# Reordering one of four attention stages and the routed gathers in a fused attention and mixture-of-experts kernel

## The chip, the cores and the metric

The kernel runs on one core of one Trainium2 chip. The metric is the device time of the whole kernel in microseconds (us), lower is better. The engines are TensorE (PE in the profile), VectorE (DVE), ScalarE (ACT), GpSimd (POOL) and SyncE (SP), which here issues nearly all DMAs. TensorE's granted clock has two levels, 1.2 and 2.4 GHz; the profile's PEclk column gives it as a share of 2.4 GHz.

## The reference

One transformer block over 2048 tokens of width 512, in float32:

```python
h = _layernorm(x) * (1 + ca) + sa
x = x + ga * attention(h)          # 16 heads of 128, causal softmax
h = _layernorm(x) * (1 + cb) + sb
# router: softmax over 64 experts, the best 4 per token, at most 128 tokens per expert
yb = silu(xb @ Wg) * (xb @ Wu) @ Wd          # per expert
x = x + gb * (sum of a token's 4 weighted expert rows + shared experts(h))
```

`sa, ca, ga, sb, cb, gb` come from a small matrix product of a conditioning vector. Two shared experts with 512 hidden columns each run over all tokens beside the routed ones.

## The kernel before, in words

**Precision.** A float32 product is made of three matmuls on a high and a low part of each operand (`matmul3`, lines 1559 to 1561). Whatever leaves PSUM therefore leaves it twice: ACT writes the high part, then DVE writes what is missing to the full value as the low part.

**Attention.** Heads run one after the other. A head has four blocks of 512 queries (j = 0 to 3), and causality gives block j the keys of blocks 0 to j. The unit of work is a stage (h, j); every engine has its own `stage` function with its orders written out by hand, and engines meet through semaphores. PE's stage (line 1649) does three things: `score(h, j)`, the logits of block j in strips of up to 512 columns (4 rows of j+1 strips, in four PSUM banks `strip`); `sum_values` of the stage before, the product of its probabilities and the values, in j+1 groups of 512 keys into the bank `pv`; and `project` for the next stage: queries, keys and values (q, k, v) into the three banks `gen`. After block 3 comes block 0 of the next head, whose stage is (h+1, 0): it holds the scores of block 0, the four-group sum of block 3 of the head before, and the projections of block 1. "The fourth block's sum" is that sum. A loop of 15 turns holds the stages (h,1), (h,2), (h,3), (h+1,0); stage (0,0) stands in front of it.

DVE's `score_row` (line 1141) takes a row of strips out of PSUM with its maximum, and ACT's `exp_row` (line 852) exponentiates it. `row_inverse` (DVE, line 1160) inverts the sum, `probs_hi` (ACT, line 858) and `probs_lo` (DVE, line 1168) make the two float16 halves of the probabilities. `gen_hi_of` (ACT, line 836) and `gen_out_of` (DVE, line 1112) take the projections out. The probabilities and the values have to be transposed for `sum_values`; that is done by DMA transposes, issued one after the other by SP (`turn_pair`, line 469, and `turn_values`, line 495).

Four orders matter around the change. (a) A pair of transposed groups goes into one of four slots of `pT`. Block 0 of a head uses slot 0, which group 2 of the fourth block's sum has to leave first: `turn_first_rows` (line 475) waits for `pv_group`, `slot_free`. (b) In SP's stage for j = 0 come the four transposes of block 0's probabilities, then `turn_values(h, 0)`, the transpose of block 0's values. (c) There is one buffer `vT16` for values before their transpose. ACT may write the values of block 1 into it only once the values of block 0 have been transposed out of it, which `gen_hi_of` says for v:

```python
act.wait_ge(v_turned, h * (16 * QB) + 16 * j)
```

(d) ACT does `gen_hi_of("v")` at the end of stage (h, 0), ahead of the exponentials of stage (h, 1), and DVE's `gen_out_of("v")` waits for it.

**After attention.** The output projection; a second layer norm; then shared-expert chunks 0 to 2 (12 steps of `shared_units`) with the router's steps beside them, given by the table `ROUTING` (line 421). Its last entry, `("table", 1)`, writes the table of routed tokens. On it wait SP's first expert weights, POOL's first gather of token rows (lines 796 to 798) and PE's first expert. 64 experts follow, with chunks 3 and 4 between them. Then come chunks 5 to 7, 12 more steps of `shared_units` (PE: gate, half of the down product of the step before, up, the other half), and beside them the combine: POOL gathers each token's four expert rows (line 811, four indirect DMAs per tile of 128 tokens, four buffers `gath`), and DVE's `combine_beside` (line 1526) adds them with their weights to the output (line 1541), two tiles in a step, in the steps that the table `COMBINE` names (line 410). PE's down product of a step waits for DVE's `shared_lo` (`hs_lo`, line 1360), which stands behind the combine of the step before on DVE.

Of the kernel before, what the change touches and what calls it, by code (L numbers as in the profile page):

```python
# [21 lines left out]
U32 = mybir.dt.uint32  # L22
ALU = mybir.AluOpType
ACT = mybir.ActivationFunctionType
AX_X = mybir.AxisListType.X
P = 128
# [15 lines left out]
def adaln_block(nc, x, Q_w, Q_b, K_w, K_b, V_w, V_b, O_w, O_b, Wr, router_bias, Wg, Wu, Wd, Sg, Su, Sd,  # L42
# [22 lines left out]
    with ExitStack() as ctx:  # L65
        def sem(name):
            return ctx.enter_context(nc.semaphore(name))
# [160 lines left out]
        slot_now = f.place("slot_now", [P, GATHS, TOPK], U32)  # L228
# [93 lines left out]
        slot_ready = sem("slot_ready")  # L322
# [83 lines left out]
        def raw_of(c):  # L406
# [3 lines left out]
        COMBINE = {step: pair for pair, step in enumerate((2, 3, 4, 6, 7, 8, 9, 10))}  # L410
# [13 lines left out]
                   11: [("table", 1)]}  # L424
# [245 lines left out]
        def _(pool):  # L670
# [133 lines left out]
            with pool.Fori(0, NT // GATHS) as g:  # L804
                for i in range(GATHS):
                    wait_alone(gath_free, g * GATHS + (i + 1))
                    nc.gpsimd.tensor_copy(slot_now[:, i, :], slot_u[:, bass.ds(g * GATHS + i, 1), :]
                                          .rearrange("p o k -> p (o k)")).then_inc(slot_ready, 1)
                    wait_alone(slot_ready, g * GATHS + (i + 1))
                    for k in range(TOPK):  # L810
                        nc.gpsimd.indirect_dma_start(
                            out=gath[i][:, k, :], out_offset=None, in_=yb_dram,
                            in_offset=bass.IndirectOffsetOnAxis(ap=slot_now[:, i, k:k + 1], axis=0)
                        ).then_inc(g_landed[i], 16)
# [3 lines left out]
        def _(act):  # L818
# [61 lines left out]
            def stage(h, j, prev, nxt):  # L880
                if nxt is not None and nxt[1] == 0:

                    act.wait_ge(gen_out, nth("v", QB - 1, h) + GENS)
                    for n in range(3):
                        act.wait_ge(raw_landed[n], h * 16 + 32)
                        if n == 2:
                            act.wait_ge(abs_ready, h + 1)
                        split_hi(n)
                exp_row(h, j, 0)
                exp_row(h, j, 1)  # L890
                probs_hi(h, j, prev, 0)
                probs_hi(h, j, prev, 1)
                exp_row(h, j, 2)
                exp_row(h, j, 3)
                probs_hi(h, j, prev, 2)
                probs_hi(h, j, prev, 3)
                if prev is not None:
                    attended(*prev)
                if j == 0:
                    take_at_scale(h)  # L900
                if nxt is not None:
                    for kind in "qkv":
                        gen_hi_of(kind, nxt[1], nxt[0])
# [156 lines left out]
        def _(dve):  # L1060
# [80 lines left out]
            def score_row(h, j, t):  # L1141
                for ch in range(j + 1):
# [31 lines left out]
            def stage(h, j, nxt):  # L1174
                score_row(h, j, 0)
                score_row(h, j, 1)
                row_inverse(h, j, 0)
                score_row(h, j, 2)
                row_inverse(h, j, 1)
                score_row(h, j, 3)  # L1180
                probs_lo(h, j, 0)
                row_inverse(h, j, 2)
                probs_lo(h, j, 1)
                row_inverse(h, j, 3)
                probs_lo(h, j, 2)
                probs_lo(h, j, 3)
                if nxt is not None:
                    hn, jn = nxt
                    gen_out_of("q", jn, hn)
                    gen_out_of("k", jn, hn)  # L1190
                    if jn == 0:
                        value_scale(hn, pv[:, 0:1])
                    gen_out_of("v", jn, hn)
# [335 lines left out]
            def combine_beside(step):  # L1529

                if step not in COMBINE:
                    return
                pair = (2 * COMBINE[step], 2 * COMBINE[step] + 1)
                dve.wait_ge(down_out, OUT_AFTER + step // (SC - AFTER0) * TB)
                for k in range(TOPK):
                    for t in pair:
                        if k == 0:
                            dve.wait_ge(g_landed[t % GATHS], (t // GATHS + 1) * 16 * TOPK)
                        else:
                            dve.wait_ge(dve_step, steps[0] - 1)  # L1540
                        ins = nc.vector.scalar_tensor_tensor(acc[:, t, :], gath[t % GATHS][:, k, :],  # L1541
                                                             w_top[:, t, k:k + 1], acc[:, t, :], ALU.mult, ALU.add)
                        steps[0] += 1
                        ins.then_inc(dve_step, 1)
                dve.wait_ge(dve_step, steps[0])
                dve.sem_inc(combined, 2)
                dve.sem_inc(gath_free, 2)
# [8 lines left out]
        def _(pe):  # L1556
# [81 lines left out]
            def stage(h, j, prev, nxt):  # L1638
                score(h, j)
                if prev is not None:  # L1640
# [4 lines left out]
                if nxt is not None:  # L1645
                    hn, jn = nxt
                    project("q", jn, hn)
                    project("k", jn, hn)
# [263 lines left out]
```

## Time and profile before

| | us |
|---|---|
| median of 3 runs | 2115.48 (2110.93 to 2117.49) |
| profiled execution, own time | 2119.06 |
| its span | 2117.3 |
| PE busy | 2014.0 (95%) |
| DVE busy | 1381.3 (65%) |
| ACT busy | 1103.8 (52%) |
| POOL busy | 386.7 (18%) |

Attention takes the span from about 70 to 1375 us, the output projection goes on to 1590, chunks 0 to 2 with the router to 1700, the experts to 1988, chunks 5 to 7 with the combine to the end. In a timeline a row gives start, duration, engine, line and operation, output and inputs with their shapes, and in brackets how long the engine sat idle before it and what ended that. Matmuls are pipelined: one of 512 columns is shown with some 0.39 us but the next starts 0.23 us later, so start to start is the thing to read. In a table of stretches the number in brackets behind a busy time is the number of instructions.

### The profile page before, as it was taken

To read this page: it belongs to the slowest core of one execution; us is meant where nothing else is said; L and a number is where in the kernel's file an instruction comes from. 1 tells how busy PE (TensorE), PEld (TensorE's weight loads), DVE (VectorE), ACT (ScalarE), POOL (GpSimd) and SP (SyncE) were. 2 spreads that over 40 slices of the span, in tenths; PEclk is the share of its full clock that TensorE was granted. 3 is DMA by queue.
4 is the path that set the end of the run, shared out by engine and by line. 5 is a ranking of instruction groups with operands and counts; after the bars stand their busy time and mean duration, and the time that the engine had idled before them with its cause. 6 is when DMAs were issued, how large, how long until landed. Compare 5 with 4: busy or idle time off the path is not lost.

```text
span 2117.3 us, 33076 instructions
## 1 busy us (share of the span) xinstructions
PE 2014.0 (95%) x9863; PEld 1501.2 (71%) x9865; DVE 1381.3 (65%) x3219; ACT 1103.8 (52%) x1638; POOL 386.7 (18%) x409
## 2 busy tenths in 40 slices
PE   6899999999999999999999999999999989999997
PEld 4667667676676677676676776667877768777775
DVE  7677686686686686776866866846545833333375
ACT  3566575676575575665766755623333134444310
POOL 5211010010110110110100101633000132222364
PEclk8999999999999999999999999999999999999998
DMA  6488888888888878878888888994431098989664
GB/s 214 95 162 161 162 162 162 162 162 161 159 165 162 173 151 171 166 156 165 162 162 161 162 161 164 214 212 151 129 106 30 1 299 286 312 279 324 187 191 152
DMA packets 932173, 366.06 MB, mean 173 GB/s; under 512 B 754800, under 2 KB 885920, under 8 KB 932128
## 3 DMA queue, kind: packets, MB, share of 16 engines
q1 hardware_dynamic: 921888, 331.93, 69.5%
q0 software_dynamic: 10240, 33.56, 5.2%
q8 instruction: 25, 0.41, 0.1%
q14 instruction: 20, 0.16, 0.0%
HBM read 138.86 MB, written 41.94 MB: 85 GB/s over the span
## 4 chain that ended last, share of the span: by engine, by line
PE 65%; SPq 15%; DMA 8%; DVE 4%; issue 4%; POOL 3%; ACT 1%; DVEq 0%; POOLq 0%; ACTq 0%
SPq L473 14%; PE gen L1559 9%; PE gen L1561 9%; PE gen L1560 9%; PE strip L1559 7%; PE strip L1560 6%; PE strip L1561 6%; PE strip L1851 4%; PE pv L1559 4%; PE pv L1561 3%; PE pv L1560 3%; DMA wd_sb<-in_L_ffn_Wd 3%; DMA pT<-p_lo 2%; PE strip L1858 2%; DVE acc L1541 1%
## 5 line engine op out<-in xcount | busy, mean ns | idle before, releaser
L1171 DVE SCALAR_TENSOR_TENSOR p_lo<-exps,rinv,p_hi 128x512 f16<-128x512 f32 (+3 forms) x256 | 395.4, 1560 | 27.9 <-ACT p_hi L864 24.3
L855 ACT ACTIVATE exps<-exps,nbias 128x128 f32<-128x128 f32 (+15 forms) x256 | 306.3, 1197 | 136.7 <-DVE nbias L1157 136.7
L864 ACT ACTIVATE p_hi<-exps,rinv 128x512 f16<-128x512 f32 (+3 forms) x256 | 338.1, 1351 | 15.1 <-DVE rinv L1166 6.7
L1559 PE MATMUL strip<-kT_hi,qT_hi 128*128 128x512 f32 (+3 forms) x640 | 238.3, 372 | 14.4 <-DVEq L1248 6.3
L1147 DVE TENSOR_SCALAR_CACHE_REDUCE exps<-strip 128x512 f32<-128x512 f32 x384 | 249.1, 685 | 1.8 <-PE strip L1561 1.8
L1559 PE MATMUL pv<-pT,v 128*128 128x512 f16 (+3 forms) x640 | 223.3, 349 | 21.0 <-DMA pT<-p_lo 19.7
L1560 PE MATMUL strip<-kT_lo,qT_hi 128*128 128x512 f32 (+3 forms) x640 | 234.4, 366 | 0.0
L1561 PE MATMUL strip<-kT_hi,qT_lo 128*128 128x512 f32 (+3 forms) x640 | 234.1, 366 | 0.0
L710 POOL TENSOR_TENSOR wq_lo<-wq_raw,wq_hi 128x512 fp32r<-128x512 f32 x16 | 20.8, 1300 | 1105.2 <-ACT wq_hi L834 1105.2
L1560 PE MATMUL pv<-pT,v 128*128 128x512 f16 (+3 forms) x640 | 222.1, 347 | 0.0
L1561 PE MATMUL pv<-pT,v 128*128 128x512 f16 (+3 forms) x640 | 218.8, 347 | 0.0
L1559 PEld LDWEIGHTS strip<-kT_hi,qT_hi 128*128 128x128 f32 x640 | 121.2, 189 | 47.0 <-DVE exps L1147 14.9
L1031 ACT ACTIVATE xbT<-gen,modT,scale_b 128x128 f32<-128x128 f32 x256 | 96.1, 456 | 92.0 <-PE gen L1843 92.0
L1559 PEld LDWEIGHTS pv<-pT,v 128*128 128x128 f16 x640 | 62.4, 97 | 114.8 <-DMA pT<-p_lo 49.2
L1561 PEld LDWEIGHTS strip<-kT_hi,qT_lo 128*128 128x128 f32 x640 | 121.3, 190 | 19.1
L1560 PEld LDWEIGHTS strip<-kT_lo,qT_hi 128*128 128x128 f32 x640 | 121.7, 190 | 15.4
L1117 DVE SCALAR_TENSOR_TENSOR qT_lo<-gen,bias_now,qT_hi 128x512 fp32r<-128x512 f32 x64 | 47.8, 746 | 126.8 <-ACT qT_hi L841 126.8
L1124 DVE SCALAR_TENSOR_TENSOR vT<-gen,v_scale,vT 128x512 f16<-128x512 f32 x64 | 48.0, 750 | 122.8 <-ACT vT L849 122.8
L1153 DVE CUSTOM_DVE_ANT_0 exps<-strip,causal 128x128 f32<-128x128 f32 (+3 forms) x256 | 124.5, 486 | 5.2 <-PE strip L1561 1.1
L1499 DVE TENSOR_TENSOR hE<-strip,sil_e 128x128 f32<-128x128 f32 x64 | 18.6, 291 | 157.2 <-ACT sil_e L1038 98.0
L849 ACT ACTIVATE vT<-gen,v_scale 128x512 f16<-128x512 f32 x64 | 44.0, 687 | 134.1 <-PE gen L1561 130.3
L1559 PE MATMUL gen<-hT_hi,a_hi 128*128 128x512 f32 x256 | 100.7, 394 | 9.1 <-DVE a_lo L1290 7.6
(237 smaller groups left out, 4433.5 us busy)
## 6 DMA issues: line engine op xcount, KB each, us to landing
at_dram<-at_f SPq DMA_DIRECT2D x64, 256.0 KB, 2.6
wg_sb<-in_L_ffn_Wg SPq DMA_DIRECT2D x64, 256.0 KB
wu_sb<-in_L_ffn_Wu SPq DMA_DIRECT2D x64, 256.0 KB
wd_sb<-in_L_ffn_Wd SPq DMA_DIRECT2D x64, 256.0 KB
yb_dram<-yb SPq DMA_DIRECT2D x64, 256.0 KB
a_f<-at_dram SPq DMA_DIRECT2D x58, 256.0 KB, 2.9
pT<-p_hi SPq DMA_TRANSPOSE x320, 3.3
pT<-p_lo SPq DMA_TRANSPOSE x320, 3.3
```

Of the source, the lines that this page charges most:

```text
L473: sp.dma_start_transpose(out, rows).then_inc(p_turned[slot_of(j, g)], 16)
L855: nc.scalar.activation(row, row, ACT.Exp, bias=nbias[:, t:t + 1], accum_out=rsum[:, t:t + 1]).then_inc(row_probs, 1)
L864: nc.scalar.activation(p_hi16[:, 0:j + 1, t, :], row, ACT.Copy, scale=rinv[:, t:t + 1]).then_inc(p_hi, 1)
L1031: ins = nc.scalar.activation(xbT[:, i % 2, P * ch:P * ch + P], e_turn[:, P * ch:P * ch + P], ACT.Identity, bias=modT[:, 3 * DC + ch:3 * DC ...
L1124: ins = nc.vector.scalar_tensor_tensor(vT16[:, 1, :], src[:], v_scale[:, 0:1], vT16[:, 0, :], ALU.mult, ALU.subtract)
L1147: nc.vector.tensor_scalar(exps[:, t, 512 * ch:512 * ch + w], strip[u % STRIPS][:, 0:w], SCALE, None, ALU.mult, ALU.max, accum_out=cmax[:, ...
L1153: nc.vector.tensor_tensor_reduce(exps[:, t, 512 * ch:512 * ch + w], strip[u % STRIPS][:, 0:w], causal[:, TB * P - w:TB * P], SCALE, -3e38, ...
L1171: nc.vector.scalar_tensor_tensor(p_lo16[:, 0:j + 1, t, :], row, rinv[:, t:t + 1], p_hi16[:, 0:j + 1, t, :], ALU.mult, ALU.subtract).then_i ...
L1559: nc.tensor.matmul(o, a_hi, b_hi, start=start, stop=False)
L1560: nc.tensor.matmul(o, a_hi, b_lo, start=False, stop=False)
L1561: return nc.tensor.matmul(o, a_lo, b_hi, start=False, stop=stop)
L1851: last = nc.tensor.matmul(e_gateup[i % 2][:, P * n:P * n + P], w[:, i % EX, c, :], xbT[:, i % 2, P * c:P * c + P], start=c == 0, stop=c == ...
```

## The change

It has four parts.

1. Stage (h, 0) on PE, ACT and DVE: q and k of block 1 are projected between the scores of block 0 and the fourth block's sum; v stays behind the sum. ACT takes q and k out ahead of its four `probs_hi`, and DVE ahead of its four `probs_lo`. SP's order is as before.
2. Stage (h, 1) on DVE: the first score row comes ahead of the low part of v of block 1 (`gen_out_of("v", 1, h)`), with a wait on `p_lo` in `score_row` for j = 1.
3. The table of routed tokens is read in step 10 instead of step 11.
4. The gathers at the end are written out tile by tile and take their indices from `slot_u` directly, without a copy to `slot_now` and a wait on it. The combine follows a new schedule from step 1 to step 10, tile by tile, each operation waiting for the one before, and frees a buffer after each tile.

```diff
-        COMBINE = {step: pair for pair, step in enumerate((2, 3, 4, 6, 7, 8, 9, 10))}
+        COMBINE = {1: (0, 1), 2: (2, 3), 3: (4,), 4: (5, 6), 5: (7, 8), 6: (9,), 7: (10, 11), 8: (12, 13), 9: (14,),
+                   10: (15,)}
...
-                   11: [("table", 1)]}
+                   10: [("table", 1)]}
...
-            with pool.Fori(0, NT // GATHS) as g:
-                for i in range(GATHS):
-                    wait_alone(gath_free, g * GATHS + (i + 1))
-                    nc.gpsimd.tensor_copy(slot_now[:, i, :], slot_u[:, bass.ds(g * GATHS + i, 1), :]
-                                          .rearrange("p o k -> p (o k)")).then_inc(slot_ready, 1)
-                    wait_alone(slot_ready, g * GATHS + (i + 1))
-                    for k in range(TOPK):
-                        nc.gpsimd.indirect_dma_start(
...
+            for t in range(NT):
+                pool.wait_ge(gath_free, t + 1)
+                for k in range(TOPK):
+                    nc.gpsimd.indirect_dma_start(
+                        out=gath[t % GATHS][:, k, :], out_offset=None, in_=yb_dram,
+                        in_offset=bass.IndirectOffsetOnAxis(ap=slot_u[:, t, k:k + 1], axis=0)
+                    ).then_inc(g_landed[t % GATHS], 16)
...
                 exp_row(h, j, 0)
                 exp_row(h, j, 1)
-                probs_hi(h, j, prev, 0)
-                probs_hi(h, j, prev, 1)
-                exp_row(h, j, 2)
-                exp_row(h, j, 3)
-                probs_hi(h, j, prev, 2)
-                probs_hi(h, j, prev, 3)
+                if j == 0:
+                    exp_row(h, j, 2)
+                    exp_row(h, j, 3)
+                    gen_hi_of("q", nxt[1], nxt[0])
+                    gen_hi_of("k", nxt[1], nxt[0])
+                    for t in range(TB):
+                        probs_hi(h, j, prev, t)
+                else:
...
                 if j == 0:
                     take_at_scale(h)
-                if nxt is not None:
+                    gen_hi_of("v", nxt[1], nxt[0])
+                elif nxt is not None:
...
             def score_row(h, j, t):
+                if j == 1:
+                    dve.wait_ge(p_lo, h * NT + (t + 1))
...
             def stage(h, j, nxt):
                 score_row(h, j, 0)
+                if j == 1:
+                    gen_out_of("v", 1, h)
                 score_row(h, j, 1)
                 row_inverse(h, j, 0)
                 score_row(h, j, 2)
                 row_inverse(h, j, 1)
                 score_row(h, j, 3)
...
+                if j == 0:
+                    row_inverse(h, j, 2)
+                    row_inverse(h, j, 3)
+                    gen_out_of("q", nxt[1], nxt[0])
+                    gen_out_of("k", nxt[1], nxt[0])
+                    probs_lo(h, j, 0)
+                    probs_lo(h, j, 1)
...
+                    if jn != 1:
+                        gen_out_of("v", jn, hn)
...
-                pair = (2 * COMBINE[step], 2 * COMBINE[step] + 1)
                 dve.wait_ge(down_out, OUT_AFTER + step // (SC - AFTER0) * TB)
-                for k in range(TOPK):
-                    for t in pair:
...
-                dve.wait_ge(dve_step, steps[0])
-                dve.sem_inc(combined, 2)
-                dve.sem_inc(gath_free, 2)
+                for t in COMBINE[step]:
+                    dve.wait_ge(g_landed[t % GATHS], (t // GATHS + 1) * 16 * TOPK)
+                    for k in range(TOPK):
+                        link(nc.vector.scalar_tensor_tensor(acc[:, t, :], gath[t % GATHS][:, k, :], w_top[:, t, k:k + 1],
+                                                            acc[:, t, :], ALU.mult, ALU.add))
+                    dve.sem_inc(combined, 1)
+                    dve.sem_inc(gath_free, 1)
...
             def stage(h, j, prev, nxt):
                 score(h, j)
+                if j == 0:
+                    project("q", *reversed(nxt))
+                    project("k", *reversed(nxt))
...
                     sum_values(hp, jp)
                 if nxt is not None:
                     hn, jn = nxt
-                    project("q", jn, hn)
-                    project("k", jn, hn)
+                    if j > 0:
+                        project("q", jn, hn)
+                        project("k", jn, hn)
```

## Rows read from the trace of the kernel before

**Rows 1.** Table of stretches, the 15 turns of the attention loop

```profile
core 0: us, PE busy (x) PEld busy (x) DVE busy (x) ACT busy (x) POOL busy (x), PEclk, DMA share, GB/s
120.00:1375.00 1255.00, 1227.60 (x5898) 883.96 (x5896) 929.11 (x2415) 804.92 (x1046) 138.00 (x116) 1.00 0.84 165
```

**Rows 2.** Timeline of PE, one stage (h, 0) and the scores behind it

```profile
639.24 0.40 PE L1561 MATMUL strip<-kT_hi,qT_lo 128*128 128x512 f32 x1
639.67 0.39 PE L1559 MATMUL pv<-pT,v 128*128 128x512 f16 x1
...
647.65 0.38 PE L1561 MATMUL pv<-pT,v 128*128 128x512 f16 x1
649.21 0.39 PE L1559 MATMUL pv<-pT,v 128*128 128x512 f16 x1 [1.18 <-DMA pT<-p_lo]
...
650.82 0.47 PE L1559 MATMUL gen<-hT_hi,wq_hi 128*128 128x512 f32 x1
...
659.09 0.39 PE L1559 MATMUL strip<-kT_hi,qT_hi 128*128 128x512 f32 x1
...
661.50 0.50 PE L1559 MATMUL strip<-kT_hi,qT_hi 128*128 128x512 f32 x1 [0.19 <-DVE exps L1147]
...
664.24 0.39 PE L1559 MATMUL pv<-pT,v 128*128 128x512 f16 x1
```

**Rows 3.** Timeline of SP's queue in the same stage, the transpose of block 0's values

```profile
654.08 1.23 SPq L499 DMA_TRANSPOSE v<-vT  x1
```

**Rows 4.** Timelines of SP, ACT and PE in stage (0, 0), by time

```profile
79.11 0.69 ACT L843 ACTIVATE kT_hi<-gen,bias_now 128x512 fp32r<-128x512 f32 x1 [1.20 <-PE gen L1561]
...
80.34 1.28 SPq L499 DMA_TRANSPOSE v<-vT  x1
...
83.50 0.69 ACT L849 ACTIVATE vT<-gen,v_scale 128x512 f16<-128x512 f32 x1 [3.71 <-DMA v<-vT]
...
85.64 0.50 PE L1559 MATMUL strip<-kT_hi,qT_hi 128*128 128x512 f32 x1 [1.79 <-DVE exps L1147]
```

**Rows 5.** DMA issues with their median us from issue to landing

```profile
at_dram<-at_f SPq DMA_DIRECT2D x64, 256.0 KB, 2.6
...
v<-vT SPq DMA_TRANSPOSE x64, 3.1
```

**Rows 6.** Timeline of PE, the first matmul behind three long waits

```profile
1426.70 0.50 PE L1559 MATMUL gen<-hT_hi,a_hi 128*128 128x512 f32 x1 [3.11 <-DVE a_lo L1290]
...
2043.77 0.79 PE L1559 MATMUL strip<-s_hi,hs_hi 128*128 128x512 f32 x1 [3.24 <-DVE hs_lo L1360]
...
2083.92 0.69 PE L1559 MATMUL strip<-s_hi,hs_hi 128*128 128x512 f32 x1 [4.06 <-DVE hs_lo L1360]
```

**Rows 7.** Table of stretches that begin at these matmuls (columns as in rows 1)

```profile
1426.70:1433.00 6.30, 4.72 (x19) 3.58 (x20) 6.23 (x7) 0.84 (x2) 6.30 (x5) 1.00 0.85 284
...
2043.80:2050.80 7.00, 7.00 (x18) 5.51 (x19) 1.38 (x2) 0.00 (x0) 4.95 (x7) 0.57 0.76 236
2083.90:2088.90 5.00, 4.98 (x15) 3.98 (x16) 0.54 (x1) 0.00 (x0) 3.58 (x5) 0.66 0.98 339
```

**Rows 8.** Timelines of DVE and PE where the table is read and the experts begin

```profile
1696.65 0.22 DVE L1479 CAST table<-strip 128x64 int32<-128x64 f32 x1
...
1704.78 0.83 PE L1843 MATMUL gen<-ident,xb 128*128 128x128 f32 x4 [4.94 <-DMA xb<-n_dram,tok_now]
```

**Rows 9.** POOL's timeline; the tile gath (ns min/median/max, first and last start us)

```profile
2088.79 0.95 POOL L811 DMA_INDIRECT gath<-yb_dram,slot_now  x1 [0.30 <-issue]
...
L811 POOL DMA_INDIRECT gath<-yb_dram,slot_now x64: 942/972/1505, 1993.9 to 2097.6; - x64
L1541 DVE SCALAR_TENSOR_TENSOR acc<-gath,w_top,acc x64: 742/744/792, 2013.6 to 2105.3; 128x512 f32<-128x512 f32 x64
```

**Rows 10.** Timeline of PE: gate of step 2, gate of step 6, last down product

```profile
2004.61 0.39 PE L1559 MATMUL strip<-h2T_hi,s_hi 128*128 128x512 f32 x1
...
2037.58 0.39 PE L1559 MATMUL strip<-h2T_hi,s_hi 128*128 128x512 f32 x1
...
2108.56 0.79 PE L1559 MATMUL strip<-s_hi,hs_hi 128*128 128x512 f32 x1 [4.79 <-DVE hs_lo L1360]
```

More of the change, by code:

```diff
@@ L227, in adaln_block @@
         ones_bf = f.place("ones_bf", [P, P], BF16)
-        slot_now = f.place("slot_now", [P, GATHS, TOPK], U32)
         tok_now = f.place("tok_now", [P, EX], I32)
@@ L321, in adaln_block @@
         yb_stored = [sem(f"yb_stored{i}") for i in range(EX)]
-        slot_ready = sem("slot_ready")
         g_landed = [sem(f"g_landed{i}") for i in range(GATHS)]
@@ L803, in _ @@
                 pool.wait_ge(yb_stored[i], 16 * (E // EX + 1))
-            with pool.Fori(0, NT // GATHS) as g:
-                for i in range(GATHS):
-                    wait_alone(gath_free, g * GATHS + (i + 1))
-                    nc.gpsimd.tensor_copy(slot_now[:, i, :], slot_u[:, bass.ds(g * GATHS + i, 1), :]
-                                          .rearrange("p o k -> p (o k)")).then_inc(slot_ready, 1)
-                    wait_alone(slot_ready, g * GATHS + (i + 1))
-                    for k in range(TOPK):
-                        nc.gpsimd.indirect_dma_start(
-                            out=gath[i][:, k, :], out_offset=None, in_=yb_dram,
-                            in_offset=bass.IndirectOffsetOnAxis(ap=slot_now[:, i, k:k + 1], axis=0)
-                        ).then_inc(g_landed[i], 16)
+            for t in range(NT):
[5 more added lines that the diff above has]
+                    ).then_inc(g_landed[t % GATHS], 16)
         @block.scalar
@@ L890, in stage @@
                 exp_row(h, j, 1)
-                probs_hi(h, j, prev, 0)
-                probs_hi(h, j, prev, 1)
-                exp_row(h, j, 2)
-                exp_row(h, j, 3)
-                probs_hi(h, j, prev, 2)
-                probs_hi(h, j, prev, 3)
+                if j == 0:
[6 more added lines that the diff above has]
+                else:
+                    probs_hi(h, j, prev, 0)
+                    probs_hi(h, j, prev, 1)
+                    exp_row(h, j, 2)
+                    exp_row(h, j, 3)
+                    probs_hi(h, j, prev, 2)
+                    probs_hi(h, j, prev, 3)
                 if prev is not None:
@@ L1180, in stage @@
                 score_row(h, j, 3)
[L1181 to L1184, printed above, removed]
+                if j == 0:
[5 more added lines that the diff above has]
+                    probs_lo(h, j, 1)
+                else:
+                    probs_lo(h, j, 0)
+                    row_inverse(h, j, 2)
+                    probs_lo(h, j, 1)
+                    row_inverse(h, j, 3)
                 probs_lo(h, j, 2)
@@ L1188, in stage @@
                     hn, jn = nxt
-                    gen_out_of("q", jn, hn)
-                    gen_out_of("k", jn, hn)
+                    if j > 0:
+                        gen_out_of("q", jn, hn)
+                        gen_out_of("k", jn, hn)
                     if jn == 0:
                         value_scale(hn, pv[:, 0:1])
-                    gen_out_of("v", jn, hn)
+                    if jn != 1:
+                        gen_out_of("v", jn, hn)
             def ln_stat_of(b):
@@ L1532, in combine_beside @@
                     return
-                pair = (2 * COMBINE[step], 2 * COMBINE[step] + 1)
                 dve.wait_ge(down_out, OUT_AFTER + step // (SC - AFTER0) * TB)
-                for k in range(TOPK):
-                    for t in pair:
[L1537 to L1544, printed above, removed]
-                dve.wait_ge(dve_step, steps[0])
-                dve.sem_inc(combined, 2)
-                dve.sem_inc(gath_free, 2)
+                for t in COMBINE[step]:
[5 more added lines that the diff above has]
+                    dve.sem_inc(gath_free, 1)
             for c in (6, 7):
@@ L1646, in stage @@
                     hn, jn = nxt
-                    project("q", jn, hn)
-                    project("k", jn, hn)
+                    if j > 0:
+                        project("q", jn, hn)
+                        project("k", jn, hn)
                     if jn == 0:
```

## The prediction

> **What bounds the kernel now.** I read the table of stretches first, then PE's timeline, then the queue that feeds it. In the attention loop PE is busy for 1227.60 of 1255 us at full clock [rows 1]: only PE's waits, some 2 us in a head, can be won there, and any new wait of PE costs in full. PE's timeline of a stage (h, 0) shows those waits. The sum of block 3 runs from 639.67 to 650.82, and in front of its last group PE waits for a transposed probability tile (1.18 us in the row; 1.34 beyond the pitch of 0.2155 us at which its matmuls follow each other); its other groups and its start wait 0.1 to 0.3 us each. The scores of block 1 then wait 0.36 us for a free strip at 661.50, because DVE had the values' low part to do first [rows 2]. At the end, chunks 5 to 7, PE waits again and again for DVE's `hs_lo`, up to 4.79 us [rows 6, 10], as DVE is in a combine that waits for gathers.
>
> **Part 1 and 2, attention.** The three waits go, about 2.1 us a head. But the projections of q and k are put ahead of the sum, so everything behind the sum is late by their time, and SP's chain is behind the sum: block 0's transposes need the slot that group 2 leaves, block 0's values come after them, and ACT may write block 1's values only when those have landed. Step by step, from the last score matmul at 639.24:
>
> - q, k and v are 36 matmuls, 650.82 to 659.09 [rows 2], 8.27 us; q and k are two thirds, 5.5, v is 2.75. Scores end at 639.47, q and k at 644.98.
> - Groups 0 to 2 of the sum: last matmul 647.65 - 639.67 = 7.98 after the first, less the small waits 0.4 [rows 2]: 7.6. So it starts at 652.58 instead of 647.65. The whole sum is 11.15 less 1.7 of waits = 9.4, and ends at 654.4. The last group's tiles, there by 649.2 [rows 2], are no longer late.
> - From that matmul to the issue of the value transpose: 654.08 - 647.65 = 6.43 [rows 2, 3], four transposes and the sequencer's steps. Nothing is taken out of it, so the issue is at 659.0. The probabilities are not what it waits for: ACT's high parts move behind k, which PE has done at 645.0, and 4 us are enough for them.
> - From issue to ACT writing block 1's values. Stage (0, 0) of this trace shows exactly this wait: 83.50 - 80.34 = 3.16, with "3.71 <-DMA v<-vT" [rows 4]. So ACT writes at 662.2; the projection of v was done at 657.2. DVE's low part stands behind it, and behind that score row 1, whose first strip is the one PE needs next.
> - From ACT's write to PE's next free strip: 85.64 - 83.50 = 2.14 [rows 4]: 664.3.
>
> PE meanwhile ran v (to 657.15) and scores: row 0 is now taken out early, so PE gets through six of eight strips, 2304 of 3328 columns of the 4.7 us that the scores take without their wait [rows 2], to 660.4, and then stands until 664.3, **3.9 us**. Two strips remain: 2.74 us from 661.50 to 664.24 for 1920 columns, so 1.46 for 1024 [rows 2]. The next sum begins at 665.8, against 664.24: **+1.5 us a head, where the waits removed are worth -2.4**. What runs behind it (ACT's and DVE's rows of block 1, about 1.7 late) keeps its distance to PE, so nothing is given back. 15 turns: **+23 us**. The bounds of this term: landing 3.0 to 3.5 instead of 3.16 and SP's reaction 0.1 shorter give +1.3 to +2.0 a head, 20 to 30 us.
>
> The Trainium skill (Advanced Engine Details and Errata, X-Bar Transpose (TRN2)) says that transposing DMAs are as fast as regular ones. Here a plain store of 256 KB lands after 2.6 us and the value transpose after 3.1 [rows 5], so the trace does not quite agree; by the page it would be 0.5 us less a head, +15 instead of +23.
>
> Stage (0, 0) has no sum in it. PE's order is the same, but ACT makes k's high part (79.11 + 0.69 [rows 4]) and only then the first two high halves, which SP's transposes follow. The value transpose, now at 80.34 [rows 4], comes about 6.4 later, at 86.7, and a PE strip follows 5.3 us behind it (85.64 - 80.34), at 92.0: 6.4 later than 85.64, of which about 1.2 come back, since two strips are left then instead of four. **+5 us**, once; bounds 3 and 8.
>
> **The clock.** A stand of 3.9 us costs more than itself. Of three waits of its size, two (3.24 and 4.06) were followed by a stretch at a granted clock of 0.57 and 0.66, that is partly at the 1.2 GHz level; the third (3.11) by 1.00 [rows 6, 7]. The time lost is 7.0 x 0.43 = 3.0 and 5.0 x 0.34 = 1.7 [rows 7]. Here the stretch behind the wait is all PE, so it is lost in full. The new wait is nearer to 4.06 than to 3.11. I take 1.8 us a head, near the row of 4.06; bounds 0 and 3.0. 15 heads and the first stage: **+29 us**, bounds 0 and 48.
>
> The wait on `p_lo` in DVE's row 0 costs nothing: the value waited for was written 8 us before by DVE itself. PSUM banks and q's registers are free in time, since scores precede the new projections on PE.
>
> **Part 3, the table.** It is read at 1696.65, after step 11's `hs_lo` [rows 8]. What it is made of is complete in step 10, and a step is 8.2 us (below): the read comes nearly 8 us earlier. PE's first expert at 1704.78 waited 4.94 us for the gathered rows [rows 8]; they come as much earlier, so the wait goes, but the sums of step 11 and ACT's split of chunk 4 are late next and keep about 1.5 us. Against it stands the half clock after that wait, about 1.7 as in the row of 2083.9 [rows 7]. **-5 us**, bounds -3 and -7; the experts behind it follow as a whole.
>
> **Part 4, gathers and combine.** Undisturbed, chunks 5 to 7 go at (2037.58 - 2004.61) / 4 = 8.24 us a step [rows 10]. Step 11 would begin at 2004.61 + 9 x 8.24 = 2078.8, its up product end 6.9 later and its low part 2.4 behind that: last down product at 2088.2 instead of 2108.56 [rows 10], and at full clock 2.8 long instead of 5.1. So at most -22.7 is to be had. A gather takes 0.95 + 0.30, at most 1.5 + 0.30 beside DVE's work, with a median near the short end [rows 9]: four to a tile are 5.0 to 5.5 without the copy and its waits, where all 64 now take 1993.9 to 2097.6, 6.5 a tile [rows 9]. The first goes some 2 us earlier without its copy; 16 tiles are issued by 2072 to 2079, and freed buffers come in time. DVE's chain costs 4 x 0.78 = 3.1 us a tile (0.744 [rows 9] and the wait for itself), two tiles 6.2 against 5.4 now. Going through the steps with 5.4 a tile, tile 8 (step 5) and tile 13 (step 8) land some 2 us after DVE wants them, and each makes PE wait about 1.8 us; the others are in time. That takes back 3.7, and 1 us more if the clock falls once: **-18 us**, bounds -22.7 and -10.
>
> **Sum.** +23 + 5 + 29 - 5 - 18 = +34 us against the profiled execution's 2119.06, which is 3.6 above the median of the runs shown. Against the median, 2115.5, the forecast is **2149 us** (+1.6%).
>
> **Rivals.** What a measurement of this kernel can tell from no change is about 0.3%, 6.3 us.
>
> (A) The forecast, chance 0.60: PE stands nearly 4 us in each stage (h, 1), with a clock drop behind most of them.
>
> (B) The same wait, but the clock holds, as it did after 3.11 us [rows 7]: +5 in all, 2120 us. Chance 0.14. For it: that one row, and that PE is dense on both sides of this wait. Against: the other two [rows 6, 7].
>
> (C) The value transpose is not late, the faster side. It decides at a landing of block 0's values by 660.4, when PE has run through its six strips, less the 2.14 of ACT and DVE: so at 658.3 instead of 662.2. If SP's transposes of block 0 did not follow group 2, they would go out from 648.3 on as now, and the waits of 2.1 + 0.3 us go: 15 x -2.4 = -36, -5, -18: 2056 us. Against it stand the wait on the slot in the code and the fact that SP starts these transposes only after group 2. Chance 0.09.
>
> (D) More of it, chance 0.17: two half-clock stretches behind each stand (the 3.0 of the 2043.8 row), or late gathers that hold PE as now, so that part 4 brings 8 instead of 18. +50 to +60, 2165 to 2175 us.
>
> **Range and chances.** From 2116, the lower edge of (B) where part 4 brings its full 22.7, to 2168, within (D); (C) and the upper part of (D) are left out. Slower by over 0.3%: (A), (D) and the half of (B) above 2122: 0.83. Within 0.3%: the rest of (B) and a little: 0.08. Faster: 0.09.
>
> **What would show it.** In the changed kernel: ACT's `vT` of block 1 ended by "DMA v<-vT" in all 16 heads, instead of once; the value transpose issued some 5 us later after the scores; a PE wait of 3.5 to 4 us in the scores of block 1, ended by DVE's `exps`, with PEclk below 1.00 in the loop's stretch; the waits for `pT` gone from the sum; a period of about 85.4 us a head instead of 82.1. The table read a step earlier, PE's first expert without its 5 us; the last down product some 20 us nearer to the first gate. I am wrong if the head's period is below 82 (then C), or if it is about 83.7 with a clock of 1.00 (then B).

## The result, and the profile after

The changed kernel takes **2163.53 us** (median of 4 runs, 2156.50 to 2167.07) where the kernel before took 2113.20 beside it: a ratio of 1.023, 95% interval 1.020 to 1.027. The forecast was 2149 (2116 to 2168), slower. Direction and range held; below it is seen that one term had the wrong sign, and another, too large, covered for it.

| profiled execution | before | after |
|---|---|---|
| time, span, us | 2119.06, 2117.3 | 2167.07, 2165.3 |
| mean granted clock | 0.989 | 0.976 |
| a head, us (ACT's `at_scale`, first to last, / 15) | 82.21 | 85.05 |
| read of the table, us | 1696.65 | 1736.68 |
| first expert's matmul, us | 1704.78 | 1748.26 |
| first gather's issue, us | 1993.9 | 2030.2 |
| last down product, us | 2108.56 | 2158.98 |

**The attention loop.** The same stretch as [rows 1], of the changed kernel (columns as there), and ACT's `at_scale`, which is written once a head (count, ns min/median/max, first to last start in us):

```profile
120.00:1375.00 1255.00, 1203.88 (x5733) 869.18 (x5732) 901.19 (x2329) 780.12 (x1022) 109.95 (x93) 0.98 0.81 158
```

```profile
L872 ACT ACTIVATE at_scale<-v_most x16: 191/203/203, 81.9 to 1357.6; 128x1 f32<-128x1 f32 x16
```

PE's busy share of the stretch falls by 24 us and the clock from 1.00 to 0.98. (1357.6 - 81.9) / 15 = 85.05 us a head. One stage (h, 0) and the scores behind it, by time: PE, then SP, then ACT and DVE of the changed kernel.

```profile
662.06 0.40 PE L1572 MATMUL strip<-kT_hi,qT_lo 128*128 128x512 f32 x1
...
683.10 0.34 PE L1572 MATMUL strip<-kT_hi,qT_lo 128*128 128x384 f32 x1
686.80 0.50 PE L1570 MATMUL strip<-kT_hi,qT_hi 128*128 128x512 f32 x1 [3.37 <-DVE exps L1153]
...
688.40 0.63 PE L1572 MATMUL strip<-kT_hi,qT_lo 128*128 128x512 f32 x1
```

```profile
675.80 1.24 SPq L472 DMA_TRANSPOSE pT<-p_hi  x1
...
679.96 1.27 SPq L472 DMA_TRANSPOSE pT<-p_lo  x1
681.56 1.23 SPq L498 DMA_TRANSPOSE v<-vT  x1
```

```profile
684.67 0.69 ACT L844 ACTIVATE vT<-gen,v_scale 128x512 f16<-128x512 f32 x1 [6.06 <-DMA v<-vT]
...
685.39 0.75 DVE L1128 SCALAR_TENSOR_TENSOR vT<-gen,v_scale,vT 128x512 f16<-128x512 f32 x1 [3.42 <-ACT vT L844]
686.06 0.68 DVE L1153 TENSOR_SCALAR_CACHE_REDUCE exps<-strip 128x512 f32<-128x512 f32 x1
```

The reader is to follow it backwards: PE's strip at 686.80 waited for DVE's `exps` of 686.06, that stood behind the values' low part, that waited for ACT's high part, and that for the transpose issued at 681.56, behind the four of the probabilities. The last of PE's rows shows the half clock: a matmul of 512 columns has a row of 0.63 us there, instead of 0.39. Two of the 15 stretches behind such a stand:

```profile
686.80:691.80 5.00, 5.00 (x19) 2.92 (x20) 4.74 (x18) 4.48 (x7) 0.00 (x0) 0.66 0.76 188
348.10:353.10 5.00, 4.99 (x26) 3.66 (x27) 4.74 (x18) 4.48 (x7) 0.00 (x0) 1.00 0.75 188
```

13 of the 15 heads look like the first (5.0 x 0.34 = 1.7 us lost), two like the second. What the waits of the whole program show of it:

```profile
DVE vT L1128 <- ACT vT L844: 150.5, 62, 6.5
DVE exps L1153 <- PE strip L1572: 132.5, 16, 8.9
ACT vT L844 <- DMA v<-vT: 99.0, 16, 7.6
PE strip L1570 <- DVE exps L1153: 57.9, 16, 6.8
PE strip L1570 <- DVE hs_lo L1378: 29.5, 5, 16.8
DVE sil_s L1374 <- remote: 26.1, 4, 11.3
ACT sil_s L990 <- remote: 14.6, 3, 7.2
```

ACT waits for the landing 16 times instead of once; PE's 57.9 us for `exps` were 4.7; PE's waits for `pT` in the sum, 19.7 us before, are gone. The last three rows belong to the end.

**The table and the end.** PE's timeline at the first expert, of the changed kernel; the 4.94 us of [rows 8] are gone:

```profile
1748.26 0.65 PE L1858 MATMUL gen<-ident,xb 128*128 128x128 f32 x4 [0.45 <-issue]
```

From the first gate's neighbourhood to the last down product the change was to save 18 us, and it lost some. Nothing of [rows 6, 10] is as long as what stands there now (timelines of PE, ACT, DVE and POOL, by time):

```profile
2049.45 0.39 PE L1572 MATMUL gen<-h2T_hi,s_lo 128*128 128x512 f32 x1
2051.86 0.69 DVE L1374 TENSOR_TENSOR sil_s<-gen,sil_s 128x512 f32<-128x512 f32 x1 [1.69 <-remote]
...
2053.62 0.39 PE L1572 MATMUL strip<-h2T_hi,s_lo 128*128 128x512 f32 x1
...
2058.06 0.39 PE L1572 MATMUL strip<-h2T_hi,s_lo 128*128 128x512 f32 x1
2059.01 0.60 ACT L990 ACTIVATE sil_s<-strip 128x512 f32<-128x512 f32 x1 [5.80 <-remote]
...
2073.27 0.95 POOL L806 DMA_INDIRECT gath<-yb_dram,slot_u  x1 [0.30 <-issue]
2074.57 0.69 DVE L1374 TENSOR_TENSOR sil_s<-strip,sil_s 128x512 f32<-128x512 f32 x1 [11.32 <-remote]
2079.43 0.77 PE L1570 MATMUL strip<-s_hi,hs_hi 128*128 128x512 f32 x1 [16.85 <-DVE hs_lo L1378]
...
2082.73 0.95 POOL L806 DMA_INDIRECT gath<-yb_dram,slot_u  x1 [8.51 <-DVEq L1558]
```

The up product's last matmul starts at 2058.06 and ACT's silu is done at 2059.6; DVE's product of the two needs nothing else and starts at 2074.57. "Remote" is the page's word for a wait whose end it can put down to nobody: the signal came, but whoever gives it had ended long before. In these 16 us POOL issues gathers 1.25 us apart (0.95 + 0.30) without a break, as it has done since 2030.2, up to 2074.2. The longer it does so, the later the signals are. PE's last matmuls in the rows end 0.39 us after their starts, at 2049.84, 2054.01 and 2058.45; the instructions that wait for them (DVE at 2051.86, ACT at 2059.01, DVE at 2074.57) start 2.0, 5.0 and 16.1 us after that. A second long wait of this kind (9.93 us) ends at 2131.65, 2.4 us after POOL's last gather. The gathers themselves are as fast as forecast.

### The profile page after: what moved, and what is told of

Read it like the earlier page. It is cut to its first block, busy times and chain, and to the rows that moved or that the text cites. A ratio compares the mean times of both kernels' runs of the same rounds, so it can differ in the third digit from the quotient of the medians.

```text
span 2165.3 us, 33071 instructions
## 1 busy us (share of the span) xinstructions
PE 2022.7 (93%) x9865; PEld 1507.4 (70%) x9865; DVE 1389.9 (64%) x3219; ACT 1103.4 (51%) x1638; POOL 381.8 (18%) x393
## 4 chain that ended last, share of the span: by engine, by line
PE 74%; SPq 7%; DMA 6%; DVE 6%; issue 2%; POOL 2%; another core or an unknown queue 1%; ACT 1%; DVEq 0%; ACTq 0%; POOLq 0%
PE gen L1570 10%; PE gen L1572 10%; PE gen L1571 10%; PE strip L1570 7%; PE strip L1572 6%; PE strip L1571 6%; SPq L472 5%; PE pv L1570 5%; PE pv L1571 5%; PE pv L1572 5%; PE strip L1866 4%; DMA v<-vT 2%; DMA wd_sb<-in_L_ffn_Wd 2%; PE strip L1873 2%; DVE acc L1555 2%
## 5 line engine op out<-in xcount | busy, mean ns | idle before, releaser
L1570 PE MATMUL strip<-kT_hi,qT_hi 128*128 128x512 f32 (+3 forms) x640 | 240.5, 376 | 67.6 <-DVE exps L1153 57.9
L1570 PE MATMUL pv<-pT,v 128*128 128x512 f16 (+3 forms) x640 | 229.9, 359 | 0.0
L1571 PE MATMUL pv<-pT,v 128*128 128x512 f16 (+3 forms) x640 | 228.6, 357 | 0.0
L1572 PE MATMUL pv<-pT,v 128*128 128x512 f16 (+3 forms) x640 | 224.4, 356 | 0.0
L1572 PEld LDWEIGHTS strip<-kT_hi,qT_lo 128*128 128x128 f32 x640 | 122.8, 192 | 19.6
L1571 PEld LDWEIGHTS strip<-kT_lo,qT_hi 128*128 128x128 f32 x640 | 122.8, 192 | 15.5
L1570 PEld LDWEIGHTS pv<-pT,v 128*128 128x128 f16 x640 | 64.6, 101 | 81.1 <-issue 22.2
L1572 PEld LDWEIGHTS pv<-pT,v 128*128 128x128 f16 x640 | 64.4, 101 | 61.3 <-issue 5.5
```

Of the source, the lines that this page charges most:

```text
L1570: nc.tensor.matmul(o, a_hi, b_hi, start=start, stop=False)
L1571: nc.tensor.matmul(o, a_hi, b_lo, start=False, stop=False)
L1572: return nc.tensor.matmul(o, a_lo, b_hi, start=False, stop=stop)
```

## The experiments

Three theories stood after the trace. **T1**: the landing of block 0's values is the new wait, SP's place behind the sum makes it late, and the half clock follows from PE's stand. **T2**: POOL's unbroken issue holds up PE's signals to DVE and ACT. **T3**, the rival to T2: the new combine, or chance. Ratios are to runs of the kernel before on the same chip, times are medians.

### Attention alone, the end alone

`attn_only` is the kernel before with the diff's attention part; `end_only` has the rest (table in step 10, COMBINE by tile, gathers written out).

> Edit: the kernel before with parts 1 and 2 (the attention's order) alone; table, gathers and combine as before. My reading of the changed kernel's trace: a head takes 85.0 us instead of 82.1, so 15 x 2.9 = 44, and the first stage some 5: 2160 to 2166 us, nothing like a 10 us stall behind 1990 us. Rival (parts 3 and 4 bring the 23 us of the forecast, and the attention costs 73): 2183 to 2190. Rival (the attention costs only what was forecast without the clock, 28): 2141.

> Edit: the kernel before with parts 3 and 4 (table a step earlier, gathers written out, combine by tile) alone; attention as before. Theory 1 (the written-out gathers, issued back to back, hold up PE's signals to ACT and DVE): PE stands for some 10 us or more at one or two places behind the first gather, ended by nothing local, as in the changed kernel; table -5, end +12: 2112 to 2125 us. Rival (those stalls come from the attention part or were chance): the forecast's -5 and -18: 2085 to 2095.

Measured: attn_only **2162.48 us**, ratio 1.022 (1.020 to 1.024); end_only **2115.08**, 1.000 (0.999 to 1.001). So the attention is worth +45 and all the rest nothing. The attention rival (+73) falls, and so does my own forecast for the end, -5 and -18. In end_only the waits are there without the attention's change:

```profile
DVE sil_s L1351 <- remote: 15.5, 4, 5.1
ACT sil_s L981 <- remote: 9.0, 2, 5.9
DVE acc L1361 <- remote: 8.7, 2, 5.8
```

attn_only has no such row. It also gives the table's own price: there the first expert's matmul still waits, and it starts at 1751.35, in the changed kernel at 1748.26.

```profile
1751.35 0.91 PE L1870 MATMUL gen<-ident,xb 128*128 128x128 f32 x4 [4.83 <-DMA xb<-n_dram,tok_now]
```

### A place of its own for block 1's values

```diff
+        vT_one = SbufMap(nc, exps_at + (3 * S + 1024) * 4).place("vT_one", [P, 2, 512], F16)
+        vT_of = [vT16, vT_one, vT16, vT16]
...
-                        act.wait_ge(v_turned, h * (16 * QB) + 16 * j)
+                    if j != 1 and not (isinstance(h, int) and h == 0 and j == 0):
+                        act.wait_ge(v_turned, h * 48 + 16 * max(0, j - 1))
...
+                if j == 2 and t == 3:
+                    dve.wait_ge(v_turned_one, h * 16 + 16)
```

> Edit: the changed kernel with a place of its own for block 1's transposed-to-be values (an idle part of exps) and a semaphore of its own, so that ACT need not wait for the landing of block 0's. Theory (that landing is the new wait, and the half clock follows from the stand): ACT's vT of block 1 is no longer ended by DMA v<-vT, PE's stand of 3.4 us in block 1's scores goes, the clock of the loop is 1.00, a head takes 79.7 to 80.3 us: 2070 to 2095 us in all. Rival (the values of block 0 are late for PE's own sum just as well): PE waits 1.5 to 3 us at the start of each first sum, ended by DMA v<-vT, a head takes 81.5 to 83.5 us: 2105 to 2135. Rival (the half clock has nothing to do with the stand): stand gone, half-clock stretches in most heads stay, about 2105.

Measured: **2085.54 us**, ratio 0.985 (0.984 to 0.987). T1 stands in its numbers; one run removes the stands of block 1's scores and the half clock behind them together. Only in stage (0, 0) does PE's first sum now wait for the landing, once, 3.8 us. The loop's stretch, `at_scale`, and the waits of vt_own:

```profile
120.00:1375.00 1255.00, 1246.95 (x6028) 908.93 (x6027) 948.94 (x2430) 814.58 (x1058) 148.02 (x122) 1.00 0.87 170
```

```profile
L875 ACT ACTIVATE at_scale<-v_most x16: 191/203/205, 82.4 to 1285.8; 128x1 f32<-128x1 f32 x16
```

```profile
ACT vT L847 <- PE gen L1577: 94.9, 47, 2.3
ACT vT_one L847 <- PE gen L1577: 23.6, 15, 1.6
```

No DMA ends ACT's wait for its values any more, and a head takes (1285.8 - 82.4) / 15 = 80.23 us: 2.0 less than before the change. That is what parts 1 and 2 have to give once the wait they call up is gone.

### SP's order, with one buffer

```diff
                 turn_first_rows(h, j)
+                if j == 0:
+                    turn_values(h, 0, h)
                 turn_last_rows(h, j)
-                if j == 0:
-                    turn_values(h, 0, h)
```

> Edit: the changed kernel, but in SP's queue of a stage (h, 0) block 0's values are transposed between the first and the last pair of probability rows, no longer behind both; one buffer as in the changed kernel. Theory (SP's place behind the sum is what makes the landing late): the issue comes 2.7 to 3 us earlier in the stage, ACT's vT is still ended by the landing but as much earlier, PE's stand shrinks from 3.4 to 0.5 to 1 us and with it the half-clock stretches go: a head at 80.6 to 81.3 us, 2088 to 2106 us in all. Rival (the probabilities moved behind it are late instead): PE waits for pT in block 0's sum, a head over 82 us, 2110 or more. Rival (a stand under 1 us still draws the half clock): a head at 82.3, 2120.

Measured: **2102.14 us**, ratio 0.994 (0.991 to 0.997). The waits of v_first:

```profile
ACT vT L844 <- DMA v<-vT: 58.5, 16, 6.0
PE strip L1570 <- DVE exps L1153: 17.4, 16, 5.2
```

Still the landing, 40 us less of it in all; of PE's 17.4 us, 5.2 are the first stage's, which leaves 0.8 a head. A head takes 81.19 us and the loop's clock is 1.00. So the place in SP's queue is the cause, and two transposes of it are nearly enough.

### Part 1 alone, part 2 alone

`part1_only` is attn_only without DVE's new order of the first row; `part2_only` the kernel before with that order alone.

> Edit: the kernel before with part 1 alone (queries and keys projected ahead of the sum; DVE takes the values' low part ahead of the first score row, as before). Theory: DVE stands behind the late values with the first row too, so PE gets four strips of block 1 instead of six before it stands; the 896 columns left over, 1.2 us, lie behind the stand: a head of 86.0 to 86.5 us, PE's stand 4.5 us, 2172 to 2190 us. Rival (part 2 is worth nothing): as with both parts, 85.0 us a head and 2160 to 2166.

> Edit: the kernel before with part 2 alone (DVE takes the first score row of block 1 ahead of the values' low part). Theory (the forecast's reading: part 1, which puts the sum and with it SP's chain behind q and k, makes the landing late; part 2 only hides it a little): ACT's vT is not ended by DMA v<-vT, the 0.36 us wait in block 1's scores goes, the values of block 1 are transposed some 2 us later, unnoticed: 2108 to 2117 us. Rival (part 2 brings a wait of its own): a head of 83 us or more, over 2125.

Measured: part1_only **2186.91 us**, ratio 1.035 (1.032 to 1.038), 86.76 us a head; part2_only **2109.36**, 0.997 (0.996 to 0.998), 81.83 us a head. The waits of part1_only:

```profile
ACT vT L849 <- DMA v<-vT: 99.1, 16, 7.7
PE strip L1579 <- DVE exps L1158: 77.9, 16, 8.4
```

ACT waits for the landing as long as with both parts (99.0), but PE stands 20 us more in all, 4.6 us a head. The head came out 0.3 over my expectation. So part 1 brings the wait, and part 2, a small gain by itself (7 us), takes some 25 us off it.

### The end: which of its edits holds the signals

`end_copy` is end_only with the old gather loop; `end_gath` is end_only with the old combine, two tiles at a time. `end_pause` and `end_sem` change the gathers of end_only by what stands ahead of each tile's four:

```diff
                 pool.wait_ge(gath_free, t + 1)
+                nc.gpsimd.tensor_copy(slot_now[:, t % GATHS, :], slot_u[:, t, :]).then_inc(slot_ready, 1)
+                pool.wait_ge(slot_ready, t + 1)
```

(end_pause; nothing reads the copy. In end_sem the copy is `pool.sem_inc(slot_ready, 1)`.)

> Edit: as the kernel before with parts 3 and 4, but with the old gather loop (a copy of a tile's slots and two waits ahead of its four gathers); the new combine by tile stays. Theory 1 (uninterrupted issue is what holds PE's signals): no wait ended by nothing local, gathers 6.3 to 6.5 us a tile, DVE waits for landings in some steps: 2095 to 2108 us. Rival (the combine's schedule is at fault): the same long stalls as with the written-out gathers, 2112 to 2125.

> Edit: the kernel before with part 3 and the written-out gathers, but the old combine, two tiles at a time. Theory 1 (it is the gathers): waits ended by nothing local again, though the old combine frees tiles later and so breaks POOL's issue more often: 2105 to 2120 us. Rival (only the new combine makes the stalls): none, DVE waits for landings as in the kernel before, 2100 to 2106.

> Edit: the kernel before with parts 3 and 4, gathers written out by tile and taking their slots where they lie, but with a copy of a few bytes that nothing needs, and a wait for it, ahead of each tile's four gathers. Theory 1 (PE's signals are held while POOL issues without a break): no PE stand of 10 us, no wait ended by nothing local, as in the run with the old loop: 2102 to 2110 us. Rival (it is the straight-line form of the gathers, their code or their slots read in place, not the missing break): stalls as with the change's gathers, 2112 to 2120.

> Edit: as the run with a needless copy ahead of each tile's gathers, but the copy is gone and only the wait is left, for a semaphore that POOL itself counts up just before. Reading 1 (POOL's engine must do something that is no gather, as the 0.2 us copy): the signals are held as with the change's gathers, waits ended by nothing local, 2110 to 2122 us. Reading 2 (any halt of POOL's issue, the time of a semaphore, lets them through): as with the copy, 2096 to 2106 us.

| run | gathers | combine | us | ratio | longest "remote" wait of DVE |
|---|---|---|---|---|---|
| end_only | written out | new | 2115.08 | 1.000 (0.999 to 1.001) | 5.8 |
| end_copy | old loop | new | 2109.32 | 0.996 (0.994 to 0.997) | none |
| end_gath | written out | old | 2126.32 | 1.003 (1.001 to 1.005) | 13.9 |
| end_pause | written out, copy | new | 2100.21 | 0.993 (0.991 to 0.995) | none |
| end_sem | written out, semaphore | new | 2115.34 | 1.000 (0.999 to 1.001) | 10.6 |

The medians of end_gath (2118.20 to 2134.67) and end_pause (2096.36 to 2112.30) are of all their runs; both scatter more than the others. T3 falls: the old combine with the new gathers is the worst, the new combine with the old loop has no such wait, though at 2109 it came out a little over my 2095 to 2108. Two more medians lie outside what I had expected: end_gath's 2126 (2105 to 2120) and end_pause's 2100 (2102 to 2110). In end_gath the end of a burst and the end of the wait can be read off (POOL and DVE, by time):

```profile
2051.68 0.95 POOL L805 DMA_INDIRECT gath<-yb_dram,slot_u  x1 [0.30 <-issue]
2055.13 0.69 DVE L1350 TENSOR_TENSOR sil_s<-strip,sil_s 128x512 f32<-128x512 f32 x1 [13.92 <-remote]
...
2072.86 0.94 POOL L805 DMA_INDIRECT gath<-yb_dram,slot_u  x1 [20.23 <-DVEq L1541]
```

The burst is over at 2052.6, DVE goes on at 2055.13. POOL's timeline of end_pause, two tiles' seam, then that of end_sem at the same place:

```profile
2019.65 1.11 POOL L810 DMA_INDIRECT gath<-yb_dram,slot_u  x1 [0.30 <-issue]
2020.77 0.19 POOL L807 COPY slot_now<-slot_u 128x4 uint32<-128x4 uint32 x1
2021.24 1.13 POOL L810 DMA_INDIRECT gath<-yb_dram,slot_u  x1 [0.27 <-issue]
```

```profile
2013.64 1.08 POOL L809 DMA_INDIRECT gath<-yb_dram,slot_u  x1 [0.30 <-issue]
2015.03 0.96 POOL L809 DMA_INDIRECT gath<-yb_dram,slot_u  x1 [0.30 <-DVEq L1538]
```

The semaphore alone leaves no mark: the gap is 0.30 as everywhere, and the signals are held as without it. The copy puts 0.47 us or more between two tiles' gathers, and no wait of this kind is left in the trace; two signals are still 0.7 and 1.0 us late there (DVE at 2005.82, ACT at 2028.99). In the old loop the gap between tiles is 1.01 us or more in all six kernels that have it, and their signals are taken up at once, also in the middle of a tile's four gathers. That fits T2 under both combines: what matters is not that a gather is going on, but how long POOL goes on with so little between two of them. Whether it is the 0.2 us of other work in POOL, or the longer pause, is open: no run has the one without the other.

### Together

`best` is vt_own with the old gather loop; `best2` is vt_own with end_pause's gathers.

> Edit: the changed kernel with the place of its own for block 1's values, and the old gather loop with its copies under the new combine. Both theories together: 2085.5 less the 6 us by which the old loop beat the written-out one: 2074 to 2082 us, a head at 80.2 us, no wait ended by nothing local. Rival (the gain of the old loop was chance): 2083 to 2089.

> Edit: the run best, with the gathers written out and a needless copy and a wait ahead of each tile's four, in place of the old loop. Theory: the 9 us by which that form beat the old loop under the attention of before, on top of best's 2080: 2066 to 2076 us, no wait ended by nothing local. Rival (that difference was chance): 2077 to 2083.

Measured: best **2080.00 us**, ratio 0.983 (0.981 to 0.985); best2 **2069.11**, 0.979 (0.976 to 0.982). Both beat both kernels; best2 is 2.1% faster than the kernel before. Against my expectation, best2 has waits of this kind, though none holds PE for more than 3.3 us.

```profile
ACT sil_s L997 <- remote: 9.6, 2, 5.2
DVE sil_s L1383 <- remote: 6.8, 1, 6.8
```

They are about as long as one tile's four gathers (5.4 us there), as if the copy let the signals out once a tile rather than freed them; that is a reading and no run tests it. The gathers of end_pause are written the same and its trace has no such wait, so the copy is not a sure cure; the old loop, slower by 9 and 11 us in these two pairs of kernels, is the form that never showed one.

## Why the forecast was right, and where it was not

**Right: the stand in the attention.** From the last score matmul of stage (h, 0) on, forecast against measured: value transpose issued 19.8 us later (681.56 - 662.06 = 19.5); landing to ACT 3.16 (684.67 - 681.56 = 3.11); ACT to PE's strip 2.14 (2.13); PE through six strips at 21.2 (683.3, the same); strip free at 25.1 (24.7). The stand was to be 3.9 and is 3.4, since SP came 0.3 earlier. A head was to take 85.4 and takes 85.05. Stage (0, 0) went as said: the transpose 6.2 us later, PE's strip at 91.9 where 92.0 was forecast. Rivals B and C fall with the trace: the clock did not hold, and the landing was late.

**A size off: the clock.** Forecast 1.8 us in each of 16 stages, 29 us. Measured: 1.7 in 13 of 15 heads is 22, and in the first stage the five microseconds behind the stand ran wholly at 1.2 GHz:

```profile
91.90:97.10 5.20, 5.20 (x14) 2.90 (x15) 4.94 (x19) 4.71 (x7) 0.00 (x0) 0.50 1.12 157
```

That is 2.6 more, 25 in all. With it, parts 1 and 2 were to cost 57 us; attn_only shows 45 (43 to 50 by the interval), its first expert 1751.35 - 1704.78 = 46.6. Its 15 heads hold 41.1 of that (15 x (84.95 - 82.21); in the changed kernel it is 42.6), where 15 x (1.5 + 1.8) = 49.5 were forecast. The other end of my error is stage (0, 0) with its clock, forecast 5 + 1.8: what the heads leave of the 46.6 is 5.5.

**A size off: the table.** -5 with bounds -3 and -7; 1751.35 - 1748.26 = 3.1 with the change's attention, 3.3 in end_only against before. The other runs with the attention of before and the table in step 10 start their first expert 3.4 (end_copy), 2.2 (end_pause), 2.0 (end_sem) and 0.9 us (end_gath) earlier than the kernel before, so the gain is 1 to 3.4, at or under the weak bound. PE's expert wait went, as said, but the read came 6.6 us earlier (1743.32 in attn_only, 1736.68 in the changed kernel) where nearly 8 were forecast. The stretch from the first expert to the gates of chunk 5 is 5 to 7 us shorter in the changed kernel and end_only, but it differs by 4 between end_only and end_copy, which are the same there, so I put it down to nothing.

**Wrong: gathers and combine.** The step that failed is "Undisturbed, chunks 5 to 7 go at 8.24 us a step" with a delay of 3.7 for two late landings. It took the copy and its waits for a pure cost of 1.0 us a tile. The gathers did run at the 5.0 to 5.5 us a tile forecast, and then PE's signals came up to 16 us late. From the first expert to the end of the span: before 412.5 us, end_only 411.7, changed kernel 417.0, end_pause 399.0. So the term was -18 and is -1 to +5 by these spans, and -13.5 with a break left in the gathers. But these spans hold the experts too, which part 4 does not touch. From ACT's first silu of chunk 5 (1995.02, 1984.94, 2033.25 and 1988.57) to the end it is 122.3, 128.3, 132.1 and 113.0 us: the term is +6 to +10, and -9 with the break, just short of the weak bound of -10. Rival D had "late gathers that hold PE as now"; the result is as large, but its mechanism was not there: in the changed kernel DVE waits for no gather's landing.

**The sum.** Forecast +57 - 5 - 18 = +34. Measured about +46 for the attention, -3 for the table, and for the end by what is left of +50, some +7. The forecast came within 15 us because 11 us too much in the attention met 25 too little at the end. That it was so near is luck; that the kernel got slower is not, since the attention alone costs 45.

## What to carry to other kernels

When work is moved ahead of a step, list what sits behind that step in every queue, the transfer queue first, and find the buffer that its landing frees: the move costs there, and a buffer of its own turned +2.3% into -1.5%, two places forward in the queue into -0.6%. A wait of some 3.4 us in the middle of dense matmuls, as in the loop here, should be priced with the half clock behind it, half as much again (1.7 us). And a copy or wait that looks like overhead between indirect DMAs may be what lets other engines' signals through: take it out in a run of its own, and compare the start of what waits with the end of what it waits for.

## What had not been expected of the hardware

**Signals held behind gathers.** In every run with gathers written out and no other work between them (changed kernel, end_only, end_gath, end_sem, vt_own, v_first), DVE and ACT waited, up to 13.9 us at a time, for signals of products that PE had finished; in the runs with the copy ahead of each tile (before, attn_only, part1_only, part2_only, end_copy, end_pause, best) the trace has no such row, and best2 alone has both. In all six, the first late signal is of a product that PE ended some 15.5 us after the first burst of gathers began: it is 0.3 to 0.5 us late. The next, at some 19.6 us, is 1.9 to 4.8 late. In the kernel before a signal takes 0.03 us or less (ACT starts at 2055.12 behind a matmul of 2054.70 to 2055.09, in the middle of a tile's gathers). The waits of more than 9 us, in five of the six, all ended 0.3 to 3.3 us after POOL's burst; shorter ones ended within a burst too. What holds the signals was not found.

**The clock.** In the loop, stands of 3.4 to 3.5 us were followed by half clock in 13 of 15 heads, those of 4.6 us in part1_only in all 15, in five of them for twice as long (the five microseconds from 525.90 are at 0.50 there, where the changed kernel has 0.66), and the 1.1 to 1.5 us waits of the kernel before in none. Between these lengths it went either way. Three five-microsecond stretches, of part1_only, of the kernel before and of v_first:

```profile
525.90:530.90 5.00, 5.00 (x13) 3.81 (x14) 4.11 (x19) 4.15 (x7) 0.00 (x0) 0.50 0.77 190
1356.10:1361.10 5.00, 4.96 (x16) 4.12 (x17) 3.18 (x10) 0.18 (x1) 4.15 (x5) 0.66 1.01 225
1342.80:1347.80 5.00, 4.97 (x25) 4.23 (x26) 4.57 (x15) 1.46 (x1) 4.18 (x5) 1.00 0.97 223
```

The second stands behind a PE wait of 2.99 us (at 1356.14, for DVE's `kT_lo`), the third behind one of 2.77 us; in vt_own a wait of 2.74 us at 1327.06 was followed by 0.67. The forecast had looked at three waits only, and took the length as its guide; with the one of 2.99 us, which its own trace has, rival B had less for it. In part1_only, the longer half-clock stretches alone add 5 x 1.7 / 15 = 0.6 us a head, against the 0.3 by which I had it too short.

**The landing.** The value transpose took 3.1 us in the changed kernel too, and a 256 KB store 2.6. The Trainium skill (Advanced Engine Details and Errata, X-Bar Transpose (TRN2)) has transposing DMAs as fast as regular ones. In this trace the two differ by 0.5 us, but a store to memory and a transpose within the core are not the same transfer, and no run has a plain copy in the transpose's place. With a landing of 2.6 the stand would have been 2.9, by my estimate from 3.4 - 0.5.
